# Seven wide sums for 28 narrow ones, ranks ahead of half of them, and six weight splits moved to the head of the expert loop

## The chip, the cores and the metric

One Trainium2 chip, one core. The metric is the device time of one execution in microseconds. A run's time is that of the whole execution; the profile's span runs from the first to the last instruction.

## The reference

A layer with two branches on the same layer norm, x of 2 x 1024 tokens by 256, float32:

```python
xn = layernorm(x)
x + attention(xn) + experts(xn)

# attention: 16 heads, 4 of keys and values; semantic and rotary parts of 32 each
pool = lambda a: concat([a[:, :, :896].reshape(B, HKV, 14, 64, d).mean(axis=3), a[:, :, 896:]], axis=2)
k_sem2, k_geo2, v2 = pool(k_sem), pool(rope(k_geo)), pool(v)      # 14 block means + 128 local keys
scores = (q_sem @ k_sem2.T + rope(q_geo) @ k_geo2.T) / sqrt(32) * exp(logit_scale)
out = softmax(where(k_pos <= pos, scores, -1e9)) @ v2 @ Wo

# experts: 16, top 4 of a softmax, weights renormalised
out = sum over the 4 chosen of w * (silu(x @ gate_e) * (x @ up_e)) @ down_e      # inner width 224
```

## The kernel before

Everything is written by hand in Bass: each engine has its own program, and semaphores join them. Nothing is scheduled by a tool, so the order in an engine's function is the order in its queue. A tile is 128 tokens; x is 16 tiles, numbered by t (0 to 7) within each of two batches.

**Norm, projections, routing (to 31 us).** DVE and ScalarE normalise x_all; PE turns each tile (`turn`) and multiplies it by the rotary keys' and the router's weights (`project`). DVE takes each token's four best experts into `chosen`.

**Stretch A (29 to 76 us).** The attention's pooled keys are means over blocks of 64 tokens. Before the change PE makes them with the tokens as stationary operand and a constant of two columns, `pool2`, as moving one: 28 matmuls in `mean_rows` for x, and four for each of seven steps in `block_means` for the rotary keys (cosine and sine halves `turned`, which DVE's `rope_k` writes and which accumulate). Then PE counts the tokens per expert with seventeen bf16 matmuls (the ranks, semaphore `ranked`). From them DVE makes `slot_i`, the row of each token and choice in a table sorted by expert, and with `weights(r)` the weight of choice r. PE repeats the keys four times (`rep_keys`), with a block sum between two of them; DVE's `rope_k(t)` waits for the block sum four steps back. POOL scatters the normalised rows into the table with 64 indirect DMAs, in four rounds r; each round waits for `weights(r)`. ScalarE empties PSUM.

**Local attention (76 to 138 us).** The last tile of each batch, eight units of one batch and four heads. DVE's `beside(n)` fits other work between them, `weights(1)` to `weights(3)` among it.

**Remote attention (to 233 us).** Seven steps t, both batches in each: PE projects and turns the queries and scores them, DVE masks and normalises, ScalarE copies the turned probabilities (`p_keep`) and takes the exponentials, SP stores the sums.

**Weights.** The experts' matmuls are made of three fp32r products, so each expert's weights are split into a high part (ScalarE, `split_high`, a cast) and a low part (`split_low`, a subtraction: experts 0 to 3 on DVE, 4 to 15 on POOL, behind its 64 scatters). SP loads experts 4 to 15 in pairs, pairs 0 to 2 after the local attention, pairs 3, 4 and 5 in remote steps 4 and 5, each at its place among the stores (`load_pair`, semaphores `w_late`). The table `SPLITS` says in which remote step ScalarE splits which experts; its eighth entry is done at the loop's head.

**Expert loop (234 us to the end).** 79 tiles of the table, software pipelined over four steps (gather and turn; gate and up; turn; down). ScalarE copies y into one of four tiles, after the scatter of four tiles before has landed; POOL adds it into out_rows with an indirect DMA. POOL's scatters stand behind its last low half. Tiles of one expert's end and the next one's beginning are kept apart by waits for landed scatters.

## Time and profile before

| | us |
|---|---|
| median of 3 runs | 454.05 (452.82 to 455.3) |
| the profiled execution | 452.22 |
| its span | 450.4 |
| PE busy in the span | 382.2 (85%) |
| POOL busy | 242.2 (54%) |
| DVE busy | 254.9 (57%) |
| ScalarE busy | 184.5 (41%) |

The profile is one execution, slightly shorter than the median. PE is TensorE, PEld its weight loads, ACT ScalarE, POOL GpSimd, SP the engine that issues most DMAs; L numbers are lines of the kernel. Each fp32 matmul of the program shows as two PE records. In brackets stands how long the engine was idle before the instruction, and what released it.

### The profile page before, as it was taken

How to read it: one execution, taken by the hardware profiler on the slowest of the kernel's cores; microseconds unless marked ns; L12 is line 12 of the kernel's file. 1: busy time of each engine (PE TensorE's matmuls, PEld its weight loads, DVE VectorE, ACT ScalarE, POOL GpSimd, SP SyncE). 2: the span in 40 equal slices, each digit the busy share in tenths (PEclk: the TensorE clock that was granted, in tenths of full speed). 3: DMA queues.
4: the chain of work that ended last, by engine and by line, in shares of the span. 5: the costliest groups of instructions: out<-in, count | busy, mean ns of one | idle time of the engine just before them, and what ended most of it. 6: DMA issues, size and time to landing. Idle time of an engine off the chain costs nothing.

```text
span 450.4 us, 8724 instructions
## 1 busy us (share of the span) xinstructions
PE 382.2 (85%) x2323; PEld 331.9 (74%) x2324; DVE 254.9 (57%) x816; ACT 184.5 (41%) x535; POOL 242.2 (54%) x211
## 2 busy tenths in 40 slices
PE   0697998888998999696436999999999999998980
PEld 0696877667985777466325999999999999887870
DVE  4785213798825999995233555555555555544430
ACT  1530104664511752114414555555555555454540
POOL 2501652465653355986325556657656666538573
PEclk9995569798999999976785999999999999999995
DMA  8990210121128943051353576676666666657543
GB/s 249 361 269 0 84 70 35 50 95 58 62 82 248 255 136 119 22 162 60 118 180 83 101 111 111 99 122 108 110 102 106 107 101 114 106 92 105 68 52 46
DMA packets 49016, 51.36 MB, mean 114 GB/s; under 512 B 5472, under 2 KB 46048, under 8 KB 48992
## 3 DMA queue, kind: packets, MB, share of 16 engines
q0 software_dynamic: 14640, 19.34, 25.9%
q1 hardware_dynamic: 34352, 31.72, 24.9%
q8 instruction: 12, 0.20, 0.2%
q14 instruction: 12, 0.10, 0.1%
HBM read 29.61 MB, written 21.43 MB: 113 GB/s over the span
## 4 chain that ended last, share of the span: by engine, by line
PE 61%; DMA 12%; DVE 11%; issue 6%; ACT 4%; SPq 2%; POOLq 2%; POOL 2%; DVEq 0%; ACTq 0%
PE bank L1224 52%; DMA out_rows<-y,idx 8%; PE bank L1576 3%; PE bank L1594 3%; DMA wdn<-in_L_ffn_down_proj 2%; POOL out_rows L637 2%; DMA x_all<-in_L_attn_x 1%; ACT x_all L659 1%; POOLq L630 1%; DVE pr L1170 1%; DVE l L1043 1%; PE bank L1236 1%; DMA out_rows<-xr 1%; DVE q L1019 1%; DVE q L1016 1%
## 5 line engine op out<-in xcount | busy, mean ns | idle before, releaser
L637 POOL DMA_INDIRECT out_rows<-y,idx x79 | 122.0, 1544 | 77.4 <-ACT y L817 39.8
L615 POOL DMA_INDIRECT xn_by_expert<-x_all,slot_i x64 | 64.8, 1012 | 20.6 <-issue 15.7
L1224 PE MATMUL bank<-wgu_hi,xh 128*128 x158 | 65.7, 416 | 5.3 <-DVE xl L1203 2.9
L1208 DVE SCALAR_TENSOR_TENSOR act<-bank,xg,sg 128x224 f32<-128x224 f32 x79 | 35.6, 451 | 55.7 <-ACT sg L804 55.5
L1224 PE MATMUL bank<-wgu_lo,xh 128*128 x158 | 59.0, 373 | 0.0
L1203 DVE TENSOR_TENSOR xl<-bank,xh 128x256 fp32r<-128x256 f32 x79 | 33.5, 425 | 44.5 <-ACT xh L795 44.5
L1224 PE MATMUL bank<-wgu_hi,xl 128*128 x158 | 58.3, 369 | 0.0
L804 ACT ACTIVATE sg<-bank 128x224 f32<-128x224 f32 x79 | 28.3, 358 | 58.9 <-PE bank L1224 58.9
L1224 PE MATMUL bank<-wdn_hi,ah 112*128 x158 | 51.3, 325 | 0.9 <-issue 0.6
L817 ACT COPY y<-bank 128x256 f32<-128x256 f32 x79 | 29.4, 373 | 38.1 <-PE bank L1224 23.4
L1224 PE MATMUL bank<-wdn_hi,al 112*128 x158 | 44.4, 281 | 0.0
L1224 PE MATMUL bank<-wdn_lo,ah 112*128 x158 | 44.2, 280 | 0.0
L601 POOL TENSOR_TENSOR wgu_lo<-wgu,wgu_hi x12 | 25.8, 2146 | 29.0 <-ACT wdn_hi L707 26.7
L612 POOL COPY x_all<-weight 128x4 f32<-128x4 f32 x16 | 4.0, 250 | 66.9 <-DVE weight L942 33.5
L1224 PEld LDWEIGHTS bank<-wgu_hi,xh 128*128 128x128 f32 x158 | 30.3, 191 | 8.3 <-issue 6.8
L1576 PE MATMUL bank<-const_k,xg 128*128 128x128 f32 x158 | 31.2, 279 | 4.9 <-DMA xg<-xn_by_expert 4.9
L795 ACT CAST xh<-bank 128x256 fp32r<-128x256 f32 x79 | 29.8, 377 | 8.9 <-PE bank L1576 8.5
L1216 DVE TENSOR_TENSOR al<-bank,ah 112x256 fp32r<-112x256 f32 x79 | 33.1, 418 | 0.8 <-ACT ah L808 0.8
L1224 PE MATMUL bank<-wqg,xT 128*128 128x512 f32 x64 | 32.6, 639 | 0.0
L1224 PEld LDWEIGHTS bank<-wgu_hi,xl 128*128 128x128 f32 x158 | 30.2, 191 | 2.7
L1224 PEld LDWEIGHTS bank<-wgu_lo,xh 128*128 128x128 f32 x158 | 30.6, 193 | 1.2
L1224 PEld LDWEIGHTS bank<-wdn_hi,ah 112*128 112x128 f32 x158 | 29.9, 189 | 1.6 <-issue 1.6
(212 smaller groups left out, 803.8 us busy)
## 6 DMA issues: line engine op xcount, KB each, us to landing
xg<-xn_by_expert SPq DMA_DIRECT2D x79, 129.0 KB, 2.4
wgu<-in_L_ffn_gate_proj SPq DMA_DIRECT2D x16, 224.0 KB, 5.1
wgu<-in_L_ffn_up_proj SPq DMA_DIRECT2D x16, 224.0 KB, 5.6
wdn<-in_L_ffn_down_proj SPq DMA_DIRECT2D x16, 224.0 KB, 6.6
x_all<-in_L_attn_x SPq DMA_DIRECT2D x8, 256.0 KB, 4.8
xr<-in_L_attn_x SPq DMA_DIRECT2D x16, 128.0 KB, 2.3
out_rows<-xr SPq DMA_DIRECT2D x16, 128.0 KB, 1.8
out_rows<-y,idx POOLq DMA_INDIRECT x79
```

Of the source, the lines that this page charges most:

```text
L601: nc.gpsimd.tensor_tensor(of_expert(wgu_l, e), of_expert(wgu, e), of_expert(wgu_h, e).bitcast(F32), ALU.subtract)
L615: gp.indirect_dma_start(xs_d, bass.IndirectOffsetOnAxis(slot_i[:, z, r:r + 1], 0), x_all[:, z, :], None).then_inc(xs_in[q], DMA)
L637: gp.indirect_dma_start(out_rows, bass.IndirectOffsetOnAxis(idx[r % RING][:, 0:1], 0), ysb[r % 4][:, :], None, compute_op=ALU.add).then_in ...
L795: nc.scalar.copy(xh[t.par][:, :, :], bank[t.par][:, 0:D].rearrange("p (c n) -> p c n", c=DC)).then_inc(xh_ready, 1)
L804: nc.scalar.activation(sg[t.par][:, :], bank[2 + t.par][:, 0:I], ACT.Silu).then_inc(sg_ready, 1)
L817: nc.scalar.copy(ysb[t.place][:, :], bank[6 + t.par][:, 0:D]).then_inc(y_ready, 1)
L1203: nc.vector.tensor_tensor(xl[t.par][:, :, :], bank[t.par][:, 0:D].rearrange("p (c n) -> p c n", c=DC), xh[t.par][:, :, :].bitcast(F32), AL ...
L1208: nc.vector.scalar_tensor_tensor(av[t.par][:, :], bank[2 + t.par][:, I:2 * I], xg[t.slot][:, D + 1:D + 2], sg[t.par][:, :], ALU.mult, ALU. ...
L1216: nc.vector.tensor_tensor(al[t.par][:, :, :], bank[4 + t.par][0:IH, 0:2 * P].rearrange("p (c n) -> p c n", c=2), ah[t.par][:, :, :].bitcas ...
L1224: return nc.tensor.matmul(o, lhsT, rhs, start=start, stop=stop)
L1576: last = nc.tensor.transpose(bank[t.par][:, c * P:(c + 1) * P], xg[t.slot][:, c * P:(c + 1) * P], ident)
L1594: last = nc.tensor.transpose(bank[4 + t.par][0:IH, c * P:(c + 1) * P], av[t.par][:, c * IH:(c + 1) * IH], ident)
```

## The change

Four edits. First, the sums: `mean_rows` and `block_means` now have the pooling columns as stationary operand, 14 columns cut out of a constant of 30 that is zero but for two (`sums_of(t)`), and stream the tokens' 512 or 256 columns; the steps accumulate, and the result has its 14 blocks on partitions. So it must be copied out of PSUM (x_mean, k_mean) and turned back by PE. Second, PE makes the ranks after the sums of steps 0 to 3, ahead of those of 4 to 6, and DVE does `rope_k(2)` and `rope_k(3)` before it waits for the ranks. Third, DVE makes `weights(1)` behind the last `rope_k` and not in `beside(0)`. Fourth, the table: experts 4 to 9 are split one remote step later, 10 to 15 at the loop's head.

```diff
-CA, NCA = columns(("below", P), ("pool", 2), ("iota_p", 1), ...
+CA, NCA = columns(("below", P), ("pools", 2 * NBLK + 2), ("iota_p", 1), ...
...
-        SPLITS = ((4, 5), (6, 7), (8, 9), (), (), (10, 11), (12, 13), (14, 15))
+        SPLITS = ((), (4, 5), (6, 7), (8, 9), (), (), (), (10, 11, 12, 13, 14, 15))
...
             act.wait_ge(means_done, 1)
+            nc.scalar.copy(x_mean[:, :, :].rearrange("p b n -> p (b n)"), bank[MEAN_BANK][0:NBLK, :]).then_inc(means_rows, 1)
+            act.wait_ge(means_turned, 1)
...
+            act.wait_ge(pooled, REMOTE)
+            nc.scalar.copy(k_mean[:, :, :].rearrange("p b n -> p (b n)"), bank[BLOCK_BANK][0:NBLK, 0:NB * KD]).then_inc(blocks_rows, 1)
             act.wait_ge(keys_turned, 1)
...
-                    act.wait_ge(w_late[5], 6 * DMA)
                     for k in SPLITS[REMOTE]:
+                        act.wait_ge(w_late[(k - EARLY) // 2], 6 * DMA)
                         split_high(k)
...
+            for t in range(2, 4):
+                rope_k(t)
+
             last_e, ends_e = bound[:, 2, :], bound[:, 3, :]
             dve.wait_ge(ranked, 1)
...
-            for t in range(2, TB):
+            for t in range(4, TB):
                 rope_k(t)
+            weights(1)
...
                 if n == 0:
                     dve.wait_ge(zeros_ready, 2)
-                    weights(1)
...
+            def sums_of(t):
+                return pools[:, NBLK - 2 * t:2 * NBLK - 2 * t]
+
             def mean_rows(t):
 
-                for b in range(NB):
-                    for c in range(DC):
-                        at = (b * DC + c) * 2 * TB + 2 * t
-                        last = mm(bank[MEAN_BANK][:, at:at + 2], x_all[:, NB * t + b, c * P:(c + 1) * P], pool2, True, True)
-                return last
+                return mm(bank[MEAN_BANK][0:NBLK, :], sums_of(t), x_all[:, NB * t:NB * (t + 1), 0:D], t == 0, t == REMOTE - 1)
...
-                for b in range(NB):
-                    at = b * 2 * TB + 2 * t
-                    for h in range(2):
-                        last = mm(bank[BLOCK_BANK][:, at:at + 2], turned[t % 4][:, h, b, :], pool2, h == 0, h == 1)
+                for h in range(2):
+                    last = mm(bank[BLOCK_BANK][0:NBLK, 0:NB * KD], sums_of(t), turned[t % 4][:, h, :, :].rearrange("p b n -> p (b n)"),
+                              t == 0 and h == 0, t == REMOTE - 1 and h == 1)
...
-            for t in range(REMOTE):
-                last = mean_rows(t)
-            last.then_inc(means_done, 1)
-
+            for t in range(4):
+                mean_rows(t)
             pe.wait_ge(chosen_ready, 1)
...
             last.then_inc(ranked, 1)
+            for t in range(4, REMOTE):
+                last = mean_rows(t)
+            last.then_inc(means_done, 1)
+            pe.wait_ge(means_rows, 1)
+            for b in range(NB):
+                for c in range(DC):
+                    at = (b * DC + c) * NBLK
+                    last = nc.tensor.transpose(bank[MEAN_BANK][:, at:at + NBLK], x_mean[:, b, c * P:(c + 1) * P], ident[0:NBLK, 0:NBLK])
+            last.then_inc(means_turned, 1)
...
+            pe.wait_ge(blocks_rows, 1)
             for b in range(NB):
+                nc.tensor.transpose(bank[BLOCK_BANK][:, b * NBLK:(b + 1) * NBLK], k_mean[:, b, :], ident[0:NBLK, 0:NBLK])
```

PE's queue in stretch A, from the last projections, before the change. The moving operand stands behind the arrow, then the stationary one; 128x2 is two moving columns.

```order
L1224 MATMUL bank<-wkr,xT_118 128x144 x4
L1224 MATMUL bank<-wkr,xT_119 128x144 x4
L1224 MATMUL bank<-wkr,xT_125 128x144 x4
L1224 MATMUL bank<-const_a,x_all 128x2 x28
L1224 MATMUL bank<-chosen,below_b 128x272
```

After it, the same place and what follows the ranks:

```order
L1235 MATMUL bank<-wkr,xT_126 128x144 x4
L1235 MATMUL bank<-x_all,const_a 14x512 x4
L1235 MATMUL bank<-chosen,below_b 128x272
L1235 MATMUL bank<-chosen,ones_b 128x256
...
L1235 MATMUL bank<-chosen,ones_b 128x16
L1235 MATMUL bank<-x_all,const_a 14x512 x3
L1298 MATMUL bank<-const_k,x_mean 128x14 x4
L1235 MATMUL bank<-turned_127,const_a 14x256 x2
L1235 MATMUL bank<-turned_128,const_a 14x256 x2
L1235 MATMUL bank<-x_keys,wk_rep 128x284 x2
```

The ranks moved ahead by three sums, and four turns of 14 columns came behind the last sum.

ScalarE's queue at the end of the remote attention and the head of the loop, before: wgu_hi and wdn_hi are the two casts of one expert's split, xh the first tiles, sg the first gate.

```order
L795 CAST xh_93<-bank 128x256
L795 CAST xh_94<-bank 128x256
L706 CAST wgu_hi<-wgu 128x896
L707 CAST wdn_hi<-wdn 112x512
L706 CAST wgu_hi<-wgu 128x896
L707 CAST wdn_hi<-wdn 112x512
L804 ACTIVATE sg_101<-bank 128x224
```

And after (the last of the splits; four more stand ahead of these, behind the two xh):

```order
L714 CAST wgu_hi<-wgu 128x896
L715 CAST wdn_hi<-wdn 112x512
L714 CAST wgu_hi<-wgu 128x896
L715 CAST wdn_hi<-wdn 112x512
L812 ACTIVATE sg_102<-bank 128x224
```

Six splits stand ahead of the first gate where two did.

## Rows read from the trace of the kernel before

**Rows 1.** The page: the chain that ended last, shares of the span by engine.

```profile
PE 61%; DMA 12%; DVE 11%; issue 6%; ACT 4%; SPq 2%; POOLq 2%; POOL 2%; DVEq 0%; ACTq 0%
```

**Rows 2.** Windows: us, busy of PE, PEld, DVE, ACT, POOL, granted clock, DMA share, GB/s.

```profile
29.16:34.30 5.14, 5.14 (x49) 5.14 (x47) 3.81 (x23) 0.42 (x1) 0.00 (x0) 0.98 0.79 184
...
45.00:61.00 16.00, 16.00 (x57) 13.82 (x57) 2.74 (x11) 1.99 (x4) 9.55 (x12) 0.50 0.22 79
...
158.00:186.00 28.00, 28.00 (x149) 21.53 (x148) 26.78 (x59) 10.06 (x27) 18.30 (x18) 1.00 0.33 109
```

**Rows 3.** Timeline, PE: start us, us, what; in brackets idle before and its releaser.

```profile
29.16 7.41 PE L1224 MATMUL bank<-const_a,x_all 128*128 128x2 f32 x56
...
36.61 2.02 PE L1224 MATMUL bank<-chosen,ones_b 128*128 128x256 bf16 x16
...
45.13 2.24 PE L1224 MATMUL bank<-x_keys,wk_rep 128*128 128x284 f32 x4
...
47.16 1.71 PE L1224 MATMUL bank<-const_a,turned 128*128 128x2 f32 x8
...
158.02 1.88 PE L1224 MATMUL bank<-wqg,xT 128*128 128x512 f32 x4
```

**Rows 4.** Timeline, DVE, ACT and PE, 38 to 77 us.

```profile
38.66 0.19 DVE L930 TENSOR_TENSOR_SCAN expert_bound<-ones,bank 128x16 f32<-128x16 f32 x1 [5.31 <-PE bank L1224]
...
42.92 0.42 DVE L882 TENSOR_TENSOR turned<-bank,const_k 128x256 f32<-128x256 f32 x1
...
63.32 0.17 ACT L695 COPY kgeo_t<-bank 128x14 f32<-128x14 f32 x1 [4.62 <-PE bank L1224]
...
76.43 0.55 PE L1224 MATMUL bank<-rep_g,qrT 32*128 32x142 f32 x8 [0.78 <-ACT qrT L714]
```

**Rows 5.** Timeline, POOL, from its first gather of weights to its first low half.

```profile
43.05 0.19 POOL L612 COPY x_all<-weight 128x4 f32<-128x4 f32 x1 [22.99 <-DVE weight L942]
...
80.62 0.19 POOL L612 COPY x_all<-weight 128x4 f32<-128x4 f32 x1 [10.47 <-DVE weight L942]
...
178.38 2.32 POOL L601 TENSOR_TENSOR wgu_lo<-wgu,wgu_hi  x1 [2.05 <-DMA xn_by_expert<-x_all,slot_i]
```

**Rows 6.** Timeline, 199 to 233 us: SP's queue, ACT, PE and DVE.

```profile
199.08 0.27 PE L1498 MATMUL bank<-const_k,pr 128*113 128x128 f32 x1
...
199.24 0.47 SPq L368 DMA_DIRECT2D wdn<-in_L_ffn_down_proj  x1
...
204.26 0.94 ACT L706 CAST wgu_hi<-wgu 128x896 fp32r<-128x896 f32 x1 [9.53 <-DMA wdn<-in_L_ffn_down_proj]
...
213.43 0.27 PE L1498 MATMUL bank<-const_k,pr 128*113 128x128 f32 x1
...
219.99 0.94 ACT L706 CAST wgu_hi<-wgu 128x896 fp32r<-128x896 f32 x1 [7.78 <-DMA wdn<-in_L_ffn_down_proj]
...
232.61 0.42 DVE L1177 TENSOR_TENSOR xr<-bank,xr 128x256 f32<-128x256 f32 x1 [0.96 <-PE bank L1224]
```

**Rows 7.** Timeline, ACT and DVE, at the head of the expert loop.

```profile
239.11 0.94 ACT L706 CAST wgu_hi<-wgu 128x896 fp32r<-128x896 f32 x1
...
244.50 1.81 DVE L1212 TENSOR_TENSOR idx<-xg,trash_row 128x1 int32<-128x1 f32 x1
...
249.39 0.37 ACT L817 COPY y<-bank 128x256 f32<-128x256 f32 x1 [0.31 <-PE bank L1224]
...
258.93 0.37 ACT L817 COPY y<-bank 128x256 f32<-128x256 f32 x1 [0.31 <-PE bank L1224]
```

**Rows 8.** Timeline, POOL, at the head of the expert loop and in it.

```profile
240.83 2.09 POOL L601 TENSOR_TENSOR wgu_lo<-wgu,wgu_hi  x1 [12.33 <-ACT wdn_hi L707]
...
244.19 2.10 POOL L601 TENSOR_TENSOR wgu_lo<-wgu,wgu_hi  x1
...
250.60 1.62 POOL L637 DMA_INDIRECT out_rows<-y,idx  x1 [3.08 <-ACT y L817]
...
271.85 1.54 POOL L637 DMA_INDIRECT out_rows<-y,idx  x1 [3.06 <-ACT y L817]
```

More of the change, by code:

```diff
@@ L83 @@
 CK, NCK = columns(("ident", P), ("cos", TB * RH), ("sin", TB * DS), ("hide", TB * NBLK), ("any", TB), ("more", TB), ("even", TB))
-CA, NCA = columns(("below", P), ("pool", 2), ("iota_p", 1), ("not_trash", NS), ("token", NT), ("slots", 4))
+CA, NCA = columns(("below", P), ("pools", 2 * NBLK + 2), ("iota_p", 1), ("not_trash", NS), ("token", NT), ("slots", 4))
 CC, NCC = columns(("heads", H), ("pair", 2), ("quad", G), ("hide_l", NKEY), ("copies", HKV * P))
@@ L178, in build @@
         prT = [wl.take(f"prT{u}", [HALF + 1, 2, P]) for u in range(NB)]
+        lpT0 = wl.take("lpT0", [P, G, P])
         wb = r_loop[1]
@@ L218, in build @@
         kgeo_t = wa.take("kgeo_t", [P, NB, NKEY])
+        x_mean = wa.take("x_mean", [NBLK, NB, D])
+        k_mean = wa.take("k_mean", [NBLK, NB, KD])
         logit = wa.take("logit", [P, NT, EX])
@@ L260, in build @@
         wv_rep = Region(oT_at[1], DC * HKV * 2 * DV * 4).take("wv_rep", [P, DC, HKV, 2, DV])
-        lpT = [wa.take(f"lpT{q}", [P, G, P]) for q in range(2)]
+        lpT = [lpT0, wa.take("lpT1", [P, G, P])]
         ws = Region(s_at, S_SIZE)
@@ L285, in build @@
         hide, any_key, more, even = (const(ck, CK, n) for n in ("hide", "any", "more", "even"))
-        below, pool2 = const(ca, CA, "below"), const(ca, CA, "pool")
+        below, pools = const(ca, CA, "below"), const(ca, CA, "pools")
         def sem(name):
@@ L299, in build @@
         xn_first, xn_second, xn_turned, xT_ready = sem("xn_first"), sem("xn_second"), sem("xn_turned"), sem("xT_ready")
-        k_raw, rope_done, pooled, means_done, means_kept = (
-            sem("k_raw"), sem("rope_done"), sem("pooled"), sem("means_done"), sem("means_kept"))
+        k_raw, rope_done, pooled, means_done, means_rows, means_turned, means_kept, blocks_rows = (
+            sem("k_raw"), sem("rope_done"), sem("pooled"), sem("means_done"), sem("means_rows"), sem("means_turned"), sem("means_kept"), sem("blocks_rows"))
         keys_turned, keys_kept = sem("keys_turned"), sem("keys_kept")
@@ L677, in _ @@
             act.wait_ge(means_done, 1)
+            nc.scalar.copy(x_mean[:, :, :].rearrange("p b n -> p (b n)"), bank[MEAN_BANK][0:NBLK, :]).then_inc(means_rows, 1)
+            act.wait_ge(means_turned, 1)
             for b in range(NB):
-                at = b * DC * 2 * TB
-                nc.scalar.copy(x_keys[:, :, b, 0:NBLK], bank[MEAN_BANK][:, at:at + DC * 2 * TB].rearrange("p (c n) -> p c n", c=DC)[:, :, 0:NBLK])
+                at = b * DC * NBLK
+                nc.scalar.copy(x_keys[:, :, b, 0:NBLK], bank[MEAN_BANK][:, at:at + DC * NBLK].rearrange("p (c n) -> p c n", c=DC))
                 last = nc.scalar.copy(x_keys[:, :, b, NBLK:NKEY], xT[REMOTE][:, b, :, :])
@@ L692, in _ @@
                 keep_rep(n)
+            act.wait_ge(pooled, REMOTE)
+            nc.scalar.copy(k_mean[:, :, :].rearrange("p b n -> p (b n)"), bank[BLOCK_BANK][0:NBLK, 0:NB * KD]).then_inc(blocks_rows, 1)
             act.wait_ge(keys_turned, 1)
             for b in range(NB):
-                nc.scalar.copy(kgeo_t[:, b, 0:NBLK], bank[BLOCK_BANK][:, b * 2 * TB:b * 2 * TB + NBLK])
+                nc.scalar.copy(kgeo_t[:, b, 0:NBLK], bank[BLOCK_BANK][:, b * NBLK:(b + 1) * NBLK])
                 last = nc.scalar.copy(kgeo_t[:, b, NBLK:NKEY], bank[BLOCK_BANK][:, (1 + b) * P:(2 + b) * P])
@@ L1631, in constants @@
     put(a, CA, "below", p[:, None] < p[None, :])
-    put(a, CA, "pool", np.stack([p < MB, p >= MB], 1) / f(MB))
+    pools = np.zeros((P, 2 * NBLK + 2), f)
+    pools[:, NBLK:NBLK + 2] = np.stack([p < MB, p >= MB], 1) / f(MB)
+    put(a, CA, "pools", pools)
     put(a, CA, "iota_p", p)
```

## The prediction

> **What bounds the kernel now.** I read the chain that ended last first, then the granted clock by windows, then the timeline of each engine at the three places that the change touches. The chain lies 61% on TensorE and 12% on DMA [rows 1], but not on TensorE's rate alone: the reader should look at where it waits and at which of its two clocks it runs.
>
> Stretch A, 29 to 63 us: sums, ranks, keys. The 28 sums are 56 passes of two moving columns in 7.41 us, 0.132 us a pass [rows 3]; the granted clock is 1.2 GHz soon after them (0.98 of 2.4 GHz as a mean over 29.16 to 34.30, 0.50 over 45 to 61, with PE busy the whole 16 us) [rows 2]. The ranks stand behind the sums, and DVE idles 5.31 us for them, to 38.66 [rows 4]. The chain then stays on PE until ScalarE takes the turned keys at 63.32, and the local scores start at 76.43 [rows 4].
>
> Stretch B, remote attention. ScalarE waits 9.53 us and 7.78 us for the weights of experts 10, 11 and 12, 13 [rows 6], with the probabilities' copies queued behind the split. The last sum ends at 232.61 + 0.42 = 233.03.
>
> Stretch C, the loop. ScalarE begins two splits at 239.11, POOL makes the low halves from 240.83 at 3.36 us an expert (240.83 to 244.19), y of tile 0 is copied at 249.39, of tile 4 at 258.93: 2.385 us a tile. The first scatter is at 250.60 [rows 7, 8].
>
> **The change, part by part.** Times are on before's time axis; S is the shift that stretch A gains.
>
> *Sums and ranks.* Seven sums of 512 moving columns take the place of 28 of two. A call of 512 columns costs 0.86 us at 2.4 GHz: two in 1.72 (158.02 to 159.74, 1.88 with the last one's drain [rows 3], clock 1.00 in that window [rows 2]). Four before the ranks: 29.2 to 32.6. The ranks take 2.2 us at 1.2 GHz (sixteen of the seventeen in 2.02, to 38.63 [rows 3]); most of that is streamed columns, so I take 1.2 us: done at 33.9. DVE fills its idle time with two ropes of keys, 0.73 us each (0.42 for the first of three operations [rows 4]), until about 34.9. It starts on the ranks then and not at 38.66: slots are out 3.8 us earlier, near 37.7, and POOL's first copy moves from 43.05 [rows 5] to 39.2.
>
> The other three sums end at 36.5. New behind them: a copy of 512 columns (0.6, by its width from the cast of 896 in 0.94 [rows 7]), four turns of 14 columns (0.5, four light passes), the four old copies (0.9, by width). The means are kept at 39.2, which hides beside the first two block sums (37.9 to 39.7).
>
> *Block sums.* Two calls of 256 columns take the place of eight passes of two. At 1.2 GHz that is no gain: 4 x 256 columns twice are the same 1.71 us that the row shows for eight passes. At 2.4 GHz it is 0.86. A repeated key and a block sum take 3.60 us now (45.13 to 48.73, with 2.03 to 47.16 for the keys [rows 3]); at 2.4 GHz 1.0 + 0.86. Four of these from 39.7 end at 47.1, the last block sum at 48.0, the new copy and turns add 2 us: the keys are turned at 50.0, where they were at 63.3. S is 13.3, plus 0.7 because the 512-column queries that follow begin at 1.2 GHz today: 14. All of it hangs on the clock. I take off 1 us for a stretch at 1.2 GHz around the one gap (36.5 to 37.9), so **S = 13**. If the clock stays at 1.2 GHz, 3.6 us a step return, and S is 1 to 2: what the slots gain is lost to the added copy and turns. Those are the two ends.
>
> The Trainium skill ("TensorE: Matmul & The Clock Gate", LDWEIGHTS) puts a weight load at its columns over 1.2 GHz. By it a pass of two columns behind 128 stationary ones costs 107 ns, and a 14-column load next to nothing. The 132 ns of the row agree in kind, and the sum goes by the rows.
>
> *Weights of round 1 ahead of local attention.* POOL idles 10.47 us at 80.62 for them [rows 5]. Made at about 46 they are there before POOL wants them (39.2 plus a round's 27.1, as 43.05 to 80.62 less 10.47: 66). POOL's 64 scatters therefore end 14 us earlier, near 164 and not 178; its low halves of experts 4 to 9 start with them. As the attention shifts by S too, the two meet in the same phase. At S = 1 they meet earlier, at the same price in kind.
>
> *Splits.* Experts 10 to 13 leave the attention, and 4 to 9 move one step later, onto weights that are there. At the first wait the turned probabilities had been there at 199.35 and were copied from 205.6: 6.1 us. At the second they were there at 213.7 and copied from 221.4: 7.6 us [rows 6]. The second expert of each step stood between the two exponentials: 1.3 us each. Sum 16.3; I take 16 and the attention ends at 217.0. Why not the full 9.53 + 7.78: PE and DVE had their own work in the first part of both waits.
>
> *The head.* The first tiles come 16 us earlier, so ScalarE begins its splits at 223.1. SP issues the last loads behind the sums of step 5, some 5 us before the attention's end: issue until 216, landing 5.0 later as at 199.24 to 204.26 [rows 6], 221. Six splits take 9.3 us (0.94 for the larger cast and 0.61), to 232.4, and y of tile 0 is there at about 238.5. POOL starts 1.72 after ScalarE, as now (239.11 to 240.83 [rows 7, 8]), at 224.8, and needs 6 x 3.36 = 20.2: 245.0. All scatters stand behind that. The signal to the first costs 0.84 (y 249.39 + 0.37 to 250.60): 245.9. There are four y tiles: tile 4 waits for scatter 0 to land. A scatter at a boundary between experts starts 1.54 + 3.06 = 4.6 after the one before it [rows 8], which is my price of landing. So y of tile 4 is at 250.5 (PE alone would allow 238.5 + 9.5 = 248.0), against 258.93: **8.4 us gained**, half of the 16 given back. From there the loop runs as before: PE's 2.385 a tile first, then POOL's chain.
>
> One cost hides there. DVE's idx takes 1.81 us at 244.50 and ends at 246.31, just when POOL's subtraction of 244.19 + 2.10 does [rows 7, 8]. With six low halves this happens for some five tiles, up to 1.8 us each. It is free as long as tile 4 waits for POOL; without that cover it costs 1 to 4 us. The Trainium skill ("SBUF — State Buffer", Who interferes with whom) says that a DVE instruction with two SBUF inputs contends with a GpSimd one that reads SBUF; by that rule, the trace agrees, and the other three operations of a tile, with one input in PSUM, don't wait.
>
> **Sum.** The profiled execution took 452.22 us around its span of 450.4. 452.22 - 13 - 8.4 = 430.8. The median of the runs, 454.05, is 1.8 above that execution, the lowest 1.4 below the median; I forecast 431.5.
>
> **The rivals.**
> 1. *The clock stays low.* For it: the stationary operand is now 14 columns wide, and no row shows whether such a stream holds the clock; alternating full and light work at 45 to 61 did not raise it. Against: PE now streams without the two-column passes that preceded the fall. Then S = 1.5: 442.5.
> 2. *The head holds more.* If idx delays or the late loads hit tile 4, the 8.4 shrink to 4: 435. If POOL's low halves don't hold it at all, 10.5: 428.5. Both lie near the forecast.
> 3. *Slower.* POOL's six subtractions stand ahead of every scatter. If they and DVE's work blocked each other in turn, the scatter chain would start late. With S = 13 it starts at 232.9 in my sum, against 250.60; an expert's low half would have to cost 3.36 + 17.7/6 = 6.3 us to eat the lead, and at 7 us the kernel takes 456. The 3.36 us at the head, with DVE's idx in it, speaks against it.
> 4. *The change doesn't do what it says:* the loads of experts 12 to 15 are issued behind sums that something else keeps late, and the wait only moves to the loop. The 8.4 fall to nothing with S = 1.5: 450.5.
>
> **How the numbers follow.** Forecast 0.62, the clock rival 0.22, the head's variants 0.08, slower 0.03, no effect 0.05. The range goes from 426 (S = 14, the head 11, 1 us of a better clock in the local attention) to the clock rival's 443. The forecast alone: 427 to 436. Half a per cent, 2.3 us, is about what these runs can tell from no change. Faster 0.94, same 0.03, slower 0.03.
>
> **What would show it.** After: the granted clock near 1.00 through 38 to 50 us; sums of 0.86 us; local scores starting near 62.5 and not 76.43; POOL's second round not waiting for DVE; no wait for expert weights on ScalarE in the attention; six splits in a row; first scatter near 233, with POOL busy before it and y of tile 4 released by a DMA. Wrong is the forecast if the clock falls to 1.2 GHz under 14-column sums, or if y of tile 4 comes later than about 240.

## The result, and the profile after

The changed kernel takes 430.99 us, median of four runs (430.14 to 431.69), beside 454.68 us for the kernel before on the same chip (452.82 to 459.6): ratio 0.946, with a 95% interval from 0.939 to 0.954 (the two medians alone give 0.948). The forecast was 431.5. A few executions fell in a slower state of the chip, and they are left out of all ratios and, in experiments 11 and 12 below, of the medians and ranges (439.99 and 428.12 us). The profiled execution has a span of 429.8 us where it was 450.4, and its mean granted clock is 0.953 of 2.4 GHz where it was 0.905.

First the granted clock, by the same windows as in [rows 2], and one window at the loop's head.

```profile
29.16:34.30 5.14, 5.14 (x30) 2.10 (x28) 4.72 (x28) 0.42 (x1) 0.00 (x0) 1.00 0.76 179
...
45.00:61.00 16.00, 15.46 (x75) 10.11 (x74) 5.55 (x14) 4.93 (x13) 8.74 (x11) 1.00 0.21 74
...
210.00:220.00 10.00, 6.21 (x18) 4.58 (x18) 1.06 (x3) 9.39 (x17) 6.98 (x5) 0.56 0.21 54
```

Over 45 to 61 us PE was granted 0.50 [rows 2], and is granted 1.00 now. The reader should compare the same work in both: the four records of a repeated key took 2.24 us [rows 3]. The timeline of PE in stretch A shows what they take now: 1.23.

```profile
29.62 3.60 PE L1235 MATMUL bank<-x_all,const_a 128*14 128x512 f32 x8
...
33.28 1.12 PE L1235 MATMUL bank<-chosen,ones_b 128*128 128x256 bf16 x16
...
38.10 1.90 PE L1235 MATMUL bank<-turned,const_a 128*14 128x256 f32 x8
39.93 1.23 PE L1235 MATMUL bank<-x_keys,wk_rep 128*128 128x284 f32 x4
...
63.82 0.55 PE L1235 MATMUL bank<-rep_g,qrT 32*128 32x142 f32 x8 [0.78 <-ACT qrT L722]
```

A float32 product counts two here, so x8 are four calls. Four sums of x take 3.60 us, sixteen of the seventeen matmuls of the ranks 1.12 (2.02 before), and the local scores start at 63.82 and not 76.43 [rows 4]: 12.61 us earlier. DVE, ACT and POOL beside it, to be read against [rows 4, 5]:

```profile
35.08 0.17 DVE L941 TENSOR_TENSOR_SCAN expert_bound<-ones,bank 128x16 f32<-128x16 f32 x1
...
39.45 0.19 POOL L616 COPY x_all<-weight 128x4 f32<-128x4 f32 x1 [19.16 <-DVE weight L953]
...
51.56 0.17 ACT L703 COPY kgeo_t<-bank 128x14 f32<-128x14 f32 x1 [1.82 <-issue]
...
68.95 0.19 POOL L616 COPY x_all<-weight 128x4 f32<-128x4 f32 x1 [1.82 <-DMA xn_by_expert<-x_all,slot_i]
...
161.79 2.09 POOL L605 TENSOR_TENSOR wgu_lo<-wgu,wgu_hi  x1 [2.16 <-DMA xn_by_expert<-x_all,slot_i]
```

DVE starts on the ranks 3.58 us earlier, POOL scatters 3.60 us earlier and no longer waits for DVE at its second round; its low halves begin at 161.79 and not 178.38. Now the end of the attention: its last sum on DVE, SP's queue, and PE's first turn of a token tile.

```profile
201.48 0.42 DVE L1188 TENSOR_TENSOR xr<-bank,xr 128x256 f32<-128x256 f32 x1 [0.44 <-PE bank L1235]
...
201.97 0.47 SPq L372 DMA_DIRECT2D wdn<-in_L_ffn_down_proj  x1
...
204.79 7.04 SPq L561 DMA_DIRECT2D xg<-xn_by_expert  x7
...
209.83 1.11 PE L1594 MATMUL bank<-const_k,xg 128*128 128x128 f32 x4 [8.39 <-DMA xg<-xn_by_expert]
```

The last sum ends at 201.90, where it was 233.03 [rows 6]. No split waits for weights in between. But here stands a wait that the prediction had too short: PE idles 8.39 us for the gather of tile 0 (4.46 before), which SP issued behind the last expert's load. Two parts make the difference. SP issues the gather 2.89 us after the last sum and not 1.80 (234.83 less 233.03), and PE starts 5.04 us after that and not 2.20 (237.03 less 234.83), while the loads issued just ahead are still moving: the DMA share is 1.04 over 204 to 210, where it was 0.30 over 233 to 238. Last the loop's head, the rows that answer to [rows 7, 8]:

```profile
226.35 0.37 ACT L825 COPY y<-bank 128x256 f32<-128x256 f32 x1 [0.49 <-PE bank L1235]
...
234.74 0.38 ACT L825 COPY y<-bank 128x256 f32<-128x256 f32 x1 [1.31 <-PE bank L1235]
...
237.95 0.37 ACT L825 COPY y<-bank 128x256 f32<-128x256 f32 x1 [1.13 <-DMA out_rows<-y,idx]
...
239.50 0.38 ACT L825 COPY y<-bank 128x256 f32<-128x256 f32 x1 [0.31 <-PE bank L1235]
```

```profile
212.97 2.12 POOL L605 TENSOR_TENSOR wgu_lo<-wgu,wgu_hi  x1 [29.18 <-ACT wdn_hi L715]
...
233.37 1.62 POOL L641 DMA_INDIRECT out_rows<-y,idx  x1
```

Six low halves fill POOL from 212.97 to 233.23; the first scatter starts 0.14 later. The `y` shown are those of tiles 0, 3, 4 and 5. From y of tile 4 to the end of the span it is 191.9 us, and was 191.5 (450.4 less 258.93): the loop behind it hardly changed. So all of the gain stands ahead of 237.95, and this sum tells where: tile 4's y is 20.98 us earlier; 12.61 of it came by the local scores, 18.52 more by the attention's end (233.03 - 201.90 - 12.61), and 10.15 were given back between there and tile 4.

### The profile page after: what moved, and what is told of

It is laid out like the page before. It is cut to its first block, busy times and chain, and to the rows that moved or that the text cites. A ratio compares the mean times of both kernels' runs of the same rounds, so it can differ in the third digit from the quotient of the medians.

```text
span 429.8 us, 8599 instructions
## 1 busy us (share of the span) xinstructions
PE 366.6 (85%) x2259; PEld 307.9 (72%) x2260; DVE 252.8 (59%) x816; ACT 186.3 (43%) x537; POOL 242.8 (56%) x211
## 4 chain that ended last, share of the span: by engine, by line
PE 62%; DVE 12%; DMA 9%; issue 6%; ACT 4%; SPq 3%; POOLq 2%; POOL 1%; another core or an unknown queue 0%; DVEq 0%; ACTq 0%
PE bank L1235 52%; DMA out_rows<-y,idx 6%; PE bank L1594 3%; PE bank L1612 3%; ACT wgu_hi L714 1%; DMA xg<-xn_by_expert 1%; DMA x_all<-in_L_attn_x 1%; DVE l L1055 1%; ACT x_all L663 1%; PE bank L1359 1%; POOL out_rows L641 1%; DVE idx L1223 1%; DVE lmax L1058 1%; PE bank L1247 1%; DVE q L1028 1%
## 5 line engine op out<-in xcount | busy, mean ns | idle before, releaser
L619 POOL DMA_INDIRECT xn_by_expert<-x_all,slot_i x64 | 65.9, 1029 | 20.4 <-issue 15.7
L1612 PE MATMUL bank<-const_k,act 128*112 128x128 f32 x158 | 30.3, 273 | 1.9 <-DVE act L1219 1.9
L1235 PE MATMUL bank<-wqg,xT 128*128 128x512 f32 x64 | 31.7, 623 | 0.0
```

What stands on the lines that cost most here:

```text
L619: gp.indirect_dma_start(xs_d, bass.IndirectOffsetOnAxis(slot_i[:, z, r:r + 1], 0), x_all[:, z, :], None).then_inc(xs_in[q], DMA)
L1235: return nc.tensor.matmul(o, lhsT, rhs, start=start, stop=stop)
L1612: last = nc.tensor.transpose(bank[4 + t.par][0:IH, c * P:(c + 1) * P], av[t.par][:, c * IH:(c + 1) * IH], ident)
```

## The experiments

Twelve kernels, in four groups. The ratio of each is to the kernel before, run beside it in the same group; the kernels are compared among each other by their medians. The medians of the kernel before went from 452.3 to 456.1 us from group to group, and the changed kernel's own runs stand beside none of the four. So a microsecond or two between kernels of different groups (experiments 1, 2, 5, 6; 3, 4, 7, 8; 9, 10, 11; 12) can be shown by a trace, but not by the times.

**1. The splits alone.** The kernel before with the new table and the wait moved into the loop of the head:

```diff
-        SPLITS = ((4, 5), (6, 7), (8, 9), (), (), (10, 11), (12, 13), (14, 15))
+        SPLITS = ((), (4, 5), (6, 7), (8, 9), (), (), (), (10, 11, 12, 13, 14, 15))
```

> The kernel before with the new table of splits alone (experts 4 to 9 a step later, 10 to 15 at the loop's head). My theory: the two waits in the remote attention go (16 us there), and about half is given back at the head, because POOL makes six low halves ahead of its first scatter: 443 to 447 against 454.7 of before, the first scatter some 4 to 7 us after the sixth split ends, y of tile 4 released by a scatter. Rival: the table is worth nothing without the earlier start of the attention (the loads of experts 10 to 15 stay late and the head waits for them): 452 to 455.

Measured: 444.1 us (442.07 to 447.55), ratio 0.984 (0.976 to 0.992). The last sum of the attention ends at 214.83, 18.2 us earlier than before, and the first scatter starts at 244.73 rather than 250.60. The clock over 45 to 61 stays at 0.50 and POOL waits 10.47 us for DVE as before. So this part alone gains some 10 us of span (8 by the medians of its group), and it has both sides in it: 18 gained in the attention, 8 given back at the head. Part of the 18 is the clock. The last eight matmuls of an attention step, in the kernel before behind the first wait and in the changed one, where nothing waits:

```profile
206.10 3.78 PE L1224 MATMUL bank<-vw,prT 112*128 112x256 f32 x8 [3.44 <-ACT prT L765]
```

```profile
194.87 1.96 PE L1235 MATMUL bank<-vw,prT 112*128 112x256 f32 x8
```

In the last three steps of the kernel before these eight take 3.78, 3.69 and 3.30 us, and in experiment 1 they take 1.96, 1.96 and 2.00: 4.9 us less. The waits for weights cost the clock too.

**2. All but the splits.** The changed kernel with the old table:

> The changed kernel with the old table of splits, so the sums, the ranks and the weights of round 1 alone. My theory: stretch A gives its 12.6 us whatever comes later, so 454.7 - 12.6 = 442, give or take 1.5, with ScalarE waiting 8 to 10 us twice for expert weights again. Rival: the earlier start is eaten by those waits, since the loads are issued behind the stores and other DMAs: 448 or more.

Measured: 442.5 us (440.88 to 444.24), ratio 0.979 (0.972 to 0.987); span 439.1, clock 1.00 from 29 to 61. The local scores start at 64.39. ACT waits for weights again, as in [rows 6], 11.6 to 12.1 us earlier:

```profile
192.17 0.94 ACT L714 CAST wgu_hi<-wgu 128x896 fp32r<-128x896 f32 x1 [9.78 <-DMA wdn<-in_L_ffn_down_proj]
...
208.40 0.94 ACT L714 CAST wgu_hi<-wgu 128x896 fp32r<-128x896 f32 x1 [8.28 <-DMA wdn<-in_L_ffn_down_proj]
```

The attention ends at 221.45. Spans add up: 10.1 for the splits alone, 11.3 for the rest, 20.6 for both. By medians of this group it is 8.2, 9.8 and, for the kernel of experiment 5, which is nearest the changed one, 19.4.

**3. The sums alone.** The kernel before with the pooling columns as stationary operand and nothing else (ranks behind all seven sums, `weights(1)` in `beside(0)`, the old table).

> The kernel before, with only the pooling sums turned round (pooling columns stationary, x or turned keys as 512 or 256 moving columns); ranks still behind all the x sums, the early issue of the router's weights and the list of splits as before. Theory (the clock is the gain, the order of the ranks is not): TensorE's granted clock stays at 1.00 from the sums to the local scores, the local scores start 12 to 13 us earlier, first y as much earlier, and the time is 440 to 443 us, like the run that keeps only the old list of splits. Rival (the ranks' place ahead of half the sums carries part of it): 444 us or more. The scatters' second round on GpSimd still waits for VectorE as before, since the weights(1) edit is not in.

Measured: 442.58 us (441.91 to 445.53), ratio 0.977 (0.970 to 0.983). That is the time of experiment 2: beside the old table, the ranks' place and `weights(1)` bring nothing that these times can tell. The traces do differ. The local scores start at 65.82, 10.6 us earlier than before and not 12 to 13 as expected, and 1.4 behind experiment 2; of that 0.8 is left at the end of the attention (222.24 against 221.45), and the spans are 440.6 and 439.1. The last sentence of the expectation missed as well: POOL's second round, at 70.68, waits 1.58 us for its DMA and not for DVE. Experiment 5 takes that up.

**4. The ranks late.** The changed kernel with the ranks behind all sums:

```diff
-            for t in range(4):
+            for t in range(REMOTE):
                 mean_rows(t)
             pe.wait_ge(chosen_ready, 1)
...
-            for t in range(4, REMOTE):
-                last = mean_rows(t)
```

and `rope_k(2)`, `rope_k(3)` behind the slots again.

> The changed kernel with the ranks put behind all seven x sums, and the two RoPEs of tiles 2 and 3 behind the slots, all else as changed. The slots and GpSimd's first scatter come about 2.8 us later (near 42 us rather than 39.5), and its low halves of experts 4 to 9 end near 186.5 rather than 183.8, still 25 us ahead of the head's splits. Theory (the place of the ranks is free): 430 to 432.5 us, within 0.5% of the changed kernel. Rival (VectorE's ranks now delay the keys, or GpSimd's delay reaches the head): 433.5 us or more.

Measured: 434.75 us (434.03 to 435.87), ratio 0.958 (0.953 to 0.963), 3.8 more than the changed kernel: the rival's number. The trace shows two parts of a later attention end, 206.21 for 201.90. The block sums of PE now wait 2.72 us for DVE, which has the slots first and the ropes after, and the local scores start at 65.92, 2.1 later. Most of the rest lies in the last attention step. The last eight matmuls there, of this kernel and then of the changed one:

```profile
202.18 3.57 PE L1232 MATMUL bank<-vw,prT 112*128 112x256 f32 x8 [0.22 <-ACT prT L773]
```

```profile
199.44 2.00 PE L1235 MATMUL bank<-vw,prT 112*128 112x256 f32 x8 [0.22 <-ACT prT L773]
```

The same work takes 3.57 us and 2.00 us; the granted clock over 200 to 205 is 0.74 in the one and 1.00 in the other, and PE had idled 1.66 us behind DVE just ahead in both. But not all of the 4.3 us at the attention's end goes on: PE's wait for the gather is 6.45 us instead of 8.39, tile 0 is turned 2.4 later, and the span is 3.3 longer. So the place of the ranks is worth about 2 us at the local scores; a fall of the clock that came at another moment adds 1.6 to the attention, and how much of either reaches the time isn't shown. The theory that the place is free was wrong here.

**5. `weights(1)` late.** The changed kernel with `weights(1)` back in `beside(0)`.

> The changed kernel with the weights of round 1 made after the first local scores again. My theory: the edit is nearly free of effect now: DVE has 1.3 us more in the local attention, POOL waits 0 to 2 us for them, and its 64 scatters end long before their rows are read: 431 to 432.5. Rival: POOL's order is on the path (low halves of experts 4 to 9 start later and collide with more of the attention, or the gather waits): 434 or more.

Measured: 432.91 us (430.09 to 433.7), ratio 0.955 (0.947 to 0.963), the runs overlapping those of the changed kernel; that is 0.4 above the theory's range and 1.1 below the rival's. POOL's second round starts like this:

```profile
69.06 0.19 POOL L616 COPY x_all<-weight 128x4 f32<-128x4 f32 x1 [1.77 <-DMA xn_by_expert<-x_all,slot_i]
```

It waits for its own DMA and not for DVE, whose weights were ready at 68.15, 0.9 us ahead. The edit is not what removed the 10.47 us of [rows 5]; the shift of the local attention does it, in which DVE makes these weights. What the edit is worth in time, if anything, these runs don't tell.

**6. Narrow block sums.** The changed kernel with the sums over keys as passes of two columns again (and so without the copy and the turns of k_mean), the x sums wide:

```diff
-                for h in range(2):
-                    last = mm(bank[BLOCK_BANK][0:NBLK, 0:NB * KD], sums_of(t), turned[t % 4][:, h, :, :]...,
+                for b in range(NB):
+                    at = b * 2 * TB + 2 * t
+                    for h in range(2):
+                        last = mm(bank[BLOCK_BANK][:, at:at + 2], turned[t % 4][:, h, b, :], pools[:, NBLK:NBLK + 2], h == 0, h == 1)
```

> The changed kernel with the block sums of the rotary keys in two-column passes again (and without the copy and the turns that the wide form needs), the seven sums of x wide as changed. If what holds the clock at 2.4 GHz through 38 to 50 us is the x sums and the ranks ahead of them, the light passes between the repeated keys cost nothing at that clock (8 x 0.13 = 1.06 against 1.04 us a step) and the time is 430 to 432. If the light passes bring it to 1.2 GHz, each step takes 3.6 again and not 2.1, and the queries behind run at half rate too: 437 to 441. Theory of less work alone (the clock by the way) would say no more than 1 us.

Measured: 435.88 us (435.22 to 436.39), ratio 0.964 (0.957 to 0.971), between the two numbers. PE's timeline behind the turned means:

```profile
37.95 1.95 PE L1233 MATMUL bank<-const_a,turned 128*128 128x2 f32 x16
39.76 1.26 PE L1233 MATMUL bank<-x_keys,wk_rep 128*128 128x284 f32 x4
40.81 1.71 PE L1233 MATMUL bank<-const_a,turned 128*128 128x2 f32 x8
42.37 2.24 PE L1233 MATMUL bank<-x_keys,wk_rep 128*128 128x284 f32 x4
```

The first sixteen narrow passes take 1.95 us, 0.12 a pass, and the keys behind them 1.26; then eight take 1.71, 0.21 a pass, and the same keys 2.24. The clock fell near 40.9, behind the first sixteen narrow passes and the keys after them, and it stays down beside the alternation of keys and narrow passes (0.60 as a mean over 45 to 61). The wide x sums held it until 38. The clock follows the two-column passes, not the place in the kernel. The local scores start at 69.75, 5.9 us later than in the changed kernel, and the attention ends at 208.58, 6.7 later; PE then waits 6.42 us for the gather rather than 8.39, so 4.9 of it reach the time.

**7. The gather ahead of the last loads.** In the changed kernel, SP's queue in the attention's last steps:

```diff
+                if i == REMOTE - 2:
+                    for u in range(NB):
+                        sp.wait_ge(c_rope[u], REMOTE)
+                        sp.wait_ge(c_s[u], REMOTE)
+                    for j in range(4):
+                        load_task(j, j)
                 if i >= REMOTE - 3 and i < REMOTE - 1:
                     load_pair(i)
...
-            for j in range(RING):
+            for j in range(4, RING):
                 load_task(j, j)
```

> The changed kernel with the first four gathers of sorted tokens issued on SyncE's queue ahead of the loads of the last pair of experts (14 and 15) rather than behind them. Theory (tile 0's tokens arrive late because their gather stands behind the late expert loads): tile 0 is turned at 202 to 204 us rather than 209.8, the splits of 10 to 13 follow at once, those of 14 and 15 wait for their weights until about 208 to 209, the first y comes near 219 to 220 rather than 226.35, and the time is 423 to 426 us. Rival (the splits of experts 14 and 15 or GpSimd's six low halves set the head anyway): the first tile is turned early but the fourth y stays within 2 us of 234.7, time 429 us or more.

Measured: 426.76 us (425.81 to 427.81), ratio 0.940 (0.935 to 0.945): 4.2 less than the changed kernel, 0.8 above the theory's range and well below the rival's. The turn of tile 0 and ACT's wait for the last expert:

```profile
205.02 0.44 PE L1600 MATMUL bank<-const_k,xg 128*128 128x128 f32 x2 [2.45 <-DMA xg<-xn_by_expert]
```

```profile
213.08 0.94 ACT L720 CAST wgu_hi<-wgu 128x896 fp32r<-128x896 f32 x1 [0.82 <-DMA wdn<-in_L_ffn_down_proj]
```

Tile 0 comes 4.8 us earlier, a microsecond later than expected, and the split of expert 14 then waits 0.82 for its weights; the fourth y is at 229.86 rather than 234.74. The gather is issued at 201.74, ahead of the last sum's end, and PE starts 3.28 us after that. Whether the order in SP's queue or the loads still moving count for more, no run separates: the edit puts the gather ahead of both.

**8. Two splits back into the attention.** The changed kernel with 10 and 11 in the last remote step:

> The changed kernel with experts 10 and 11 split in the last remote attention step and only 12 to 15 at the loop's head. Theory (six splits in a row on ScalarE at 1.36 us each, and then six low halves on GpSimd at 3.36 us each, set when the first tiles come out): tile 0's first y comes 2.7 us earlier (near 223.6 rather than 226.35), GpSimd makes four low halves at the head and its first output scatter starts near 227 rather than 233.4, and the fourth y near 230.5 rather than 234.7; time near 427 us (426 to 428.5). Rival (ScalarE in the last attention step waits for the weights of experts 10 and 11, as before the change): the splits wait there, the attention ends later by 2 to 4 us, and the time is 430 us or more.

Measured: 429.62 us (429.37 to 430.27), ratio 0.947 (0.942 to 0.951), 1.4 less, neither number. No split waits for weights, but the attention ends at 207.94, 6 us later; the gather hides 4 of that (PE waits 4.38 for it). The weights are not the cause, and ScalarE's casts are short (0.95 and 0.63 us). With the splits POOL's low halves of 10 and 11 come into the attention (195.28 to 203.10), and DVE's work beside them is longer. Two multiplications of the last step, here and in the changed kernel, and PE behind the first of them:

```profile
200.67 2.67 DVE L1181 TENSOR_TENSOR pr<-pr,srec 128x224 f32<-128x224 f32 x2
...
202.02 0.41 PE L1515 MATMUL bank<-const_k,pr 128*112 128x128 f32 x1 [3.50 <-DVE pr L1181]
```

```profile
198.04 0.69 DVE L1181 TENSOR_TENSOR pr<-pr,srec 128x224 f32<-128x224 f32 x2
```

These and the two subtractions ahead of them are 3.5 us longer together, and the last eight matmuls, behind PE's wait, take 3.62 rather than 2.00. That is most of the 6. y of tile 0 comes at 226.03, hardly earlier, but the next follow at 2.38 us and the fourth is at 233.18.

**9. Loads and gather early.** Experiment 7, with each late pair loaded a step earlier and the gather ahead of step 5's output write.

> The changed kernel with the loads of experts 10 to 15 each issued one remote attention step earlier on SyncE's queue, and the first four gathers of sorted tokens issued in the step after the last of them, ahead of that step's output write. Theory (the head waits for what stands in SyncE's queue: first the gather, then the weights of 14 and 15): tile 0's tokens are there when the attention ends, it is turned at 202 to 204 us rather than 209.8 as changed and 205.0 with the gather alone ahead, the six splits run without a wait, the fourth y comes near 227 rather than 229.9 with the gather alone ahead, and the time is 423 to 425 us. Rival (the remaining delay is not the queue's, and the earlier loads slow the attention's own transfers): 426.5 us or more.

Measured: 425.75 us (424.72 to 427.22), ratio 0.935 (0.931 to 0.939). Tile 0 is turned at 203.69 after a wait of 0.18, the splits don't wait, y of tile 0 comes at 220.30. But the fourth y is at 228.61 rather than 227, and the fifth like this:

```profile
232.51 0.37 ACT L831 COPY y<-bank 128x256 f32<-128x256 f32 x1 [1.83 <-DMA out_rows<-y,idx]
```

With SP's queue out of the way, ACT waits 1.83 us for the first scatter, which POOL starts at 227.24, behind its six low halves. One microsecond against experiment 7 is within what the runs scatter, and the time is 0.8 above the theory's range.

**10. The same with two splits in the attention.** Experiments 8 and 9 together.

> The kernel with early loads and gather, and with experts 10 and 11 split in the last remote step rather than at the head. In the run that moved only these two splits the attention ended near 207.9 us rather than 201.9, which ate most of what the shorter head gave. Theory (a split made in that step costs the attention more than it saves the head): now that the head does not wait for its gather there is nothing for the later attention end to hide behind, and the time is the same as or above the kernel with all six at the head, by 0 to 3 us: 424 to 428 us. Rival (GpSimd's six low halves are what the head is short of): 422.5 us or less.

Measured: 423.51 us (422.54 to 425.56), ratio 0.931 (0.926 to 0.937). Neither number: 0.5 below the theory's range and 1.0 above the rival's, and the intervals of 9 and 10 overlap. The trace goes the rival's way: the attention ends 1.6 us later (205.60), but the first scatter starts at 221.31 rather than 227.24, and the tiles follow on PE's 2.38 us from the first one, the fifth y at 228.69 and not 232.51.

**11. Low halves with one input.** The changed kernel with zeros in the low halves of 10 to 15:

```diff
-            with gp.Fori(ON_DVE, E) as e:
+            with gp.Fori(ON_DVE, 10) as e:
                 split_low(e)
+            for e in range(10, E):
+                gp.wait_ge(w_hi, e + 1)
+                nc.gpsimd.tensor_scalar(of_expert(wgu_l, e), of_expert(wgu_h, e).bitcast(F32), 0.0, None, ALU.mult)
+                nc.gpsimd.tensor_scalar(of_expert(wdn_l, e), of_expert(wdn_h, e).bitcast(F32), 0.0, None, ALU.mult).then_inc(w_lo, 1)
```

> The changed kernel, but for experts 10 to 15 GpSimd fills the low halves with zeros (high half times 0.0, an instruction with one SBUF input) rather than with weight minus high half (two SBUF inputs); so the products of these experts lack their low weight halves. It measures what the two-input subtractions cost at the head. Theory (they stand ahead of the first scatter, and hold VectorE's idx operations of the first tiles): the six are done in 6 to 14 us rather than 20.3, first output scatter within 1 us behind the first y, the idx operations take 0.15 us, the fourth y comes 0.5 to 1.5 us earlier (near 233.5), and the time is 428.5 to 430.5 us: the low halves cost the loop at most 1 to 2 us. Rival (they hold the loop by the wait for the first scatter, as the prediction had it): 2.5 us or more are gained, 428 us or less.

Measured: 435.63 us (432.67 to 438.03), ratio 0.953 (0.946 to 0.960), 4.6 more and not less, so neither number; the profiled execution, 438.03, is the longest of the three. POOL, DVE and ACT at the head:

```profile
215.59 2.47 POOL L628 TENSOR_SCALAR wgu_lo<-wgu_hi 128x896 fp32r<-128x896 f32 x1 [26.89 <-ACT wdn_hi L719]
```

```profile
222.94 0.15 DVE L1227 TENSOR_TENSOR idx<-xg,trash_row 128x1 int32<-128x1 f32 x1
```

```profile
243.13 0.37 ACT L829 COPY y<-bank 128x256 f32<-128x256 f32 x1 [6.24 <-DMA out_rows<-y,idx]
```

The operation with one input is no shorter on POOL but longer, 2.45 and 1.48 us, 3.87 an expert rather than 3.36. DVE's idx beside it takes 0.15, and at most 0.62, where it took 1.68 first and 2.30 in the fifth tile, and the fourth y comes at 234.82, where it was 234.74 in the changed kernel, although the attention ends 2.0 us later. With six experts of 3.87, begun 2.6 us later, the first scatter is at 239.07, and y of tile 4 waits 6.24 us for it: 243.13 rather than 237.95. Of the 5.7 by which the scatter is late, 3.1 are the longer operations and 2.6 the later start, which the edit doesn't explain. So the wait that the prediction named is real, and here the whole delay of POOL, 5.7 us, is nearly found in y of tile 4 (5.2).

**12. Four splits in the attention.** Experiment 9 with 10, 11 in the last remote step but one, 12, 13 in the last, 14, 15 at the head: the places that the kernel before gave them.

> The kernel with early loads and gather, and with experts 10 and 11 split in the last remote step but one, 12 and 13 in the last, and only 14 and 15 at the loop's head, as the kernel before had them. Theory (the old list cost the attention its waits for weights that were loaded late, not the splits themselves): no split in the attention waits for weights now, the last x row of the attention ends 1 to 3 us later than with two splits in it (near 205.6 us there), the head is 2.7 us shorter on ScalarE, and the time is within 1.5 us of that kernel's 423.5: 422 to 425 us. Rival (splits between the attention's steps cost in themselves what the list of the kernel before cost, some 10 us for three pairs): 428 us or more.

Measured: 422.41 us (419.96 to 423.49), ratio 0.932 (0.928 to 0.936), the same as experiment 10 within the runs, and as the theory had it. The attention ends at 205.42, where 1 to 3 us more than experiment 10's 205.60 were expected; the first scatter starts at 217.22 with nothing to wait for but y. The splits that cost the kernel before some 18 us in these steps cost 1.5 now against experiment 9 (203.97), or 3.3 if the last eight matmuls are set equal, which took 1.90 us here and 3.78 there. No split waits for weights; what is left fits POOL's low halves beside DVE, as in experiment 8.

## Why the prediction was right, and where it was not

- *Clock and sums (S = 13).* Right: 12.61 at the local scores. Four sums took 3.60 us for the 3.4 forecast, the ranks 1.24 for 1.2 (33.16 to 34.40), a repeated key and a block sum 2.12 (39.93 to 42.05), for 1.86. The gaps brought no stretch at 1.2 GHz, for which 1 us had been taken off; the longer steps and a start 0.46 later took that instead. Experiments 3 and 6 show the cause: the sums alone bring 10.6 of the shift, and the two-column passes bring the fall back; the other 2 are the ranks' place (experiment 4). By the remote steps some is lost again: 11.85 (153.22 for 165.07 at the same eight matmuls).
- *Ranks.* Their place was put into the sum by its dates and not by a price. It is worth 2.1 us at the local scores in the changed kernel and 1.4 beside the old table, of which the times show nothing (experiments 2 to 4).
- *weights(1).* POOL's end was right (161.79 for 164), the cause wrong: experiment 5 has it without the edit.
- *Splits (16).* The mechanism was right, the size small: 18.5 after the shift, and 18.2 and 19.6 by experiments 1 and 2. I had counted the copies behind each wait (the first is 205.62 less 199.35, 6.27 and not 6.1) and two casts, but not that PE's work behind the waits ran at the low clock: for the last eight matmuls of three steps that alone is 4.9 us (experiment 1). It is more than the 2.5 that were missing, so some other part of the sum was too large; which, no run shows.
- *Head (half given back).* 7.6 forecast, 10.15 measured; with the term above it cancels by luck, so the sum of both, 8.4, was met (20.98 - 12.61 = 8.37). The step that failed is "ScalarE begins its splits at 223.1", 6.1 us after the attention: it took the gather's wait from before (PE idle to 237.03, from the same place to ScalarE's first split at 239.11 [rows 7]). In fact it was 9.35 us. SP issued the last loads until 202.44, half a microsecond past the attention's end and not one ahead of it, with the gather behind them, and the gather then took 5.04 us rather than 2.20. I had placed these loads and asked only when the weights land, not what is queued behind them. Experiments 7 and 9 show it: 4 to 5 us. The six splits took 8.16 us and not 9.3 (1.36 from one to the next, as at 239.11 and 240.47 in the kernel before), so y of tile 0 was only 0.85 later than the forecast's 225.5.
- *POOL's six low halves.* Right to 0.1 us (20.26 for 20.2), first scatter 233.37 for 232.9, tile 4 at 237.95 for 237.5, released by the DMA as said, 4.58 us behind the scatter for 4.6. The scatter's date had two misses that nearly cancel: POOL began at 212.97 and not 211.8, and the 0.84 us of signal, which is the way from y to a scatter, was 0.14 behind a low half. The wait also decided less than the text has it. From the fourth y PE alone would have had tile 4 at 237.1 (234.74 + 2.38), and from tile 0 at 235.9, without POOL's hold on idx; tile 5 is on PE's beat at 239.50. The late gather and POOL's queue end some two microseconds apart; experiment 9 takes the one away and finds the other, experiment 10 takes both, and experiment 11 lengthens the second and pays for it.
- *idx.* 1.68, 0.62, 0.62, 1.29 and 2.30 us in the first five tiles, each to the end of a subtraction. The last was not free:

```profile
230.95 2.30 DVE L1223 TENSOR_TENSOR idx<-xg,trash_row 128x1 int32<-128x1 f32 x1
```

  It held the work of tile 3 behind it on DVE, and y of tile 3 came 3.39 us after that of tile 2 rather than 2.38. The Trainium skill ("SBUF — State Buffer", Who interferes with whom) says that a DVE instruction with two SBUF inputs contends with a GpSimd one that reads SBUF. The changed kernel's trace agrees for subtractions. Experiment 11 does not: POOL's one-input operations read SBUF as well, and idx took 0.15 us at 222.94, inside one of them (221.92 to 223.40), and 0.62 at most. The measurement decides: what held DVE to its end here was a POOL operation with two SBUF inputs.
- *The rivals.* The clock rival is refuted by the window over 45 to 61, the slower one by 3.38 us an expert's low half (its own 456 at 7 us an expert was wrong: six times 3.64 more than 3.36 is 21.8, and 430.8 and 21.8 are 452.6), the one without effect by the splits that start at 211.25. "The head holds more" had the late loads in it, but for the weights.
- *The sum.* It starts from the profiled execution, the shortest of the kernel before (452.22), and that of the changed kernel was the longest of its four (431.69 for 430.8 forecast). The 0.5 us between 431.5 and the median is closer than the terms were, which is luck: the splits' and the head's were each off by 2.5.

Left open: when the clock falls in the last attention step. In experiments 4, 6 and 9 the last eight matmuls took 3.57, 3.66 and 3.78 us, in the changed kernel and in experiments 1, 5, 7 and 11 they took 2.00, with the same 1.66 us of idle time ahead. It costs that step 1.6 to 1.8 us, and no run here forced it; where the gather's wait stands behind, part of it is hidden.

Left standing in every kernel here: POOL's low halves of experts 4 to 9, 161.79 to 183.79 in the changed kernel, beside DVE's work in the remote attention. From one group of eight matmuls to the same of the next step it is 9.7 us (153.22 to 162.94), and across these low halves 15.9 (162.94 to 178.85). No run took them away.

## What to carry to other kernels

A sum over tokens as many two-column passes costs more than its own time: it lets the clock fall for the work behind it. Put the narrow operand on the stationary side and stream the wide one, if the result can be turned back with a few light passes. When work is moved off an engine, read the queues that it frees: the last loads ended behind the attention here and not ahead of it, and the one small gather that the next stage needs stood behind them. A split has two halves on two engines: ask what the second one, on POOL, does to DVE beside it. Where two releasers end nearly together, taking one away shows less than it is worth: experiment 9 brought tile 0 out 1.9 us earlier than experiment 7 and gained 1.0, and with POOL's queue shortened too, in experiment 10, another 2.2 followed.

## What the runs showed of the hardware

- POOL's multiplication by a constant, one input, is slower than its subtraction of two for a tile of the same size: 2.45 us for 128x896 against some 2.1, 1.48 for 112x512 against some 1.3.
- The same eight records of 256 columns took 2.00 us or 3.57 to 3.78, by the clock granted in them (1.00 over 200.57 to 202.5 in experiment 7, 0.50 over 199.73 to 203.5 in experiment 9); when a fall comes is not the same from kernel to kernel with the same instructions ahead.
- PE starts the expert loop at the low level: a matmul with the low gate weights takes 0.57 us at 222.96 and 0.37 at 226.59, with a granted clock of 0.56 over 210 to 220, after 8.39 us of idle time. An early gather does not end this (0.67 over 210 to 220 in experiment 9).
- Sixteen passes of two columns take 1.95 us at the high level and eight take 1.71 at the low one: 0.12 and 0.21 us a pass, where eight records of 256 columns take 1.90 us at the high level.
- DVE's idx, with two SBUF inputs, took 0.15 to 0.62 us beside one-input operations on POOL (experiment 11), and 0.62 to 2.30 beside subtractions with two, ending with the subtraction (the changed kernel).
